# The last stage's products as seven half-size block products instead of eight

## The reference, cut to what matters

```
def _sage_layer(h, edge_src, edge_dst, deg_inv, W_self, W_neigh, b):
    msg = h[edge_src]
    agg = segment_sum(msg, edge_dst, num_segments=h.shape[0])
    return h @ W_self + (agg * deg_inv[:, None]) @ W_neigh + b
...
h   = relu(_sage_layer(x, ..., W_self0, W_neigh0, b0))
out =      _sage_layer(h, ..., W_self1, W_neigh1, b1)
x   = _layernorm(x + out)
```

## Time and profile before

| | |
|---|---|
| median of the runs | 1059.83 us |
| profiled execution | 1060.87 us |
| its span, first to last instruction | 1059.1 us |
| TensorE busy | 999.0 us, 94% |
| VectorE busy | 516.8 us, 49% |
| ScalarE busy | 370.5 us, 35% |
| GpSimd busy | 262.4 us, 25% |
| mean granted TensorE clock | 0.983 |

### The profile page before, as it was taken

How to read it: one execution, slowest core, us unless ns; L and a number is a source line. 1 busy time by engine, 2 the same in 40 slices (tenths; PEclk the granted TensorE clock), 3 DMA queues, 4 the chain that set the end, 5 groups by cost and what they waited for, 6 DMA issues and landing times.

```text
span 1059.1 us, 14881 instructions
## 1 busy us (share of the span) xinstructions
PE 999.0 (94%) x4870; PEld 810.8 (77%) x4870; DVE 516.8 (49%) x1296; ACT 370.5 (35%) x664; POOL 262.4 (25%) x320
## 2 busy tenths in 40 slices
PE   5798899989898999999999999999999999999996
PEld 3376678879787887877777777778887777787774
DVE  7888765374667885332223332212234233235545
ACT  5687743162535576221112221113431101222221
POOL 3000003841443331633006143006116004300000
PEclk9699999999999999999999999999999999999999
DMA  6158683893013684314224014324325435104443
GB/s 204 58 97 216 171 196 73 199 204 86 0 42 121 230 287 143 104 34 149 96 75 126 22 47 135 106 104 140 114 83 159 131 109 163 29 1 132 146 146 123
DMA packets 48263, 127.13 MB, mean 120 GB/s; under 512 B 17775, under 2 KB 18784, under 8 KB 48016
## 3 DMA queue, kind: packets, MB, share of 16 engines
q1 hardware_dynamic: 33622, 74.91, 23.6%
q0 software_dynamic: 8288, 37.29, 13.3%
q10 hardware_dynamic: 6298, 14.21, 3.9%
HBM read 101.76 MB, written 45.13 MB: 139 GB/s over the span
## 4 chain that ended last, share of the span: by engine, by line
PE 77%; DVE 11%; ACT 5%; issue 3%; POOL 1%; DVEq 0%; ACTq 0%; POOLq 0%
PE bank L1778 42%; PE bank L1799 18%; PE bank L1117 6%; PE bank L1149 4%; PE bank L663 3%; PE bank L627 2%; DVE hot_keys L444 2%; ACT squares L1347 1%; DVE hot_src L443 1%; DVE dec_z L1430 1%; PE bank L1491 1%; DVE xt L475 1%; PE bank L620 1%; PE bank L1176 1%; PE bank L1476 1%
## 5 line engine op out<-in xcount | busy, mean ns | idle before, releaser
L1718 DVE TENSOR_TENSOR h_stage<-h_turned,h_stage 128x1000 fp32r<-128x1000 f32 x80 | 104.6, 1307 | 370.6 <-ACT h_stage L1643 370.6
L1778 PE MATMUL bank<-w_self,h_stage 128*125 128x512 f32 x960 | 229.5, 394 | 0.0
L1778 PE MATMUL bank<-w_neigh,h_stage 128*125 128x512 f32 x960 | 227.2, 397 | 0.0
L1778 PEld LDWEIGHTS bank<-w_self,h_stage 128*125 128x125 f32 x960 | 177.8, 185 | 45.0
L1778 PEld LDWEIGHTS bank<-w_neigh,h_stage 128*125 128x125 f32 x960 | 178.0, 186 | 43.9
L1799 PE MATMUL bank<-g_rows,a_stage 125*125 125x512 f32 x800 | 192.7, 395 | 0.0
L1643 ACT ACTIVATE h_stage<-h_turned 128x1000 fp32r (+1 forms) x80 | 84.0, 1050 | 304.6 <-PE bank L1778 293.0
L1799 PEld LDWEIGHTS bank<-g_rows,a_stage 125*125 125x125 f32 x800 | 148.4, 185 | 37.8
L1608 POOL CAST w_self<-w_stage 128x512 fp32r<-128x512 f32 x32 | 22.2, 695 | 226.3 <-PE bank L1778 218.9
L1149 PE MATMUL bank<-a_turned,gn 125*128 125x418 f32 x360 | 70.8, 354 | 3.9 <-DVE gn L1009 2.4
L1149 PEld LDWEIGHTS bank<-a_turned,gn 125*128 125x128 f32 x360 | 66.9, 188 | 5.7 <-DVE gn L1009 3.6
(11 more groups left out here) (217 smaller groups left out, 1122.6 us busy)
## 6 DMA issues: line engine op xcount, KB each, us to landing
a_stage<-at_dram SPq DMA_DIRECT2D x40, 625.0 KB, 4.0
w_stage<-w_self POOLq DMA_DIRECT2D x32, 256.0 KB, 3.1
at_dram<-a_turned SPq DMA_DIRECT2D x10, 625.0 KB, 9.6
w_stage<-w_neigh POOLq DMA_DIRECT2D x24, 256.0 KB, 2.9
dec_y<-x_bd SPq DMA_DIRECT2D x10, 512.0 KB, 3.7
dec_x<-x_ob SPq DMA_DIRECT2D x10, 512.0 KB, 4.6
x_dram<-h_rows SPq DMA_DIRECT2D x10, 512.0 KB, 2.9
h_dram<-o ACTq DMA_DIRECT2D x20, 256.0 KB
```

What stands on the lines that cost most here:

```text
L1718: dve.tensor_tensor(st[u][:, 1, :, :], ht[:, :, bass.ds(t * NT, NT)], raw(st[u][:, 0, :, :]), ALU.subtract).then_inc(st_ready, 1)
L1778: mm = pe.matmul(out, st[u][:, a, k, :], w[:, b, k * 512:(k + 1) * 512], start=(k == 0 and p == 0), stop=(k == KD - 1 and p == 2))
```

## The change

For one quarter, write h in row halves (tiles 0 to 4, tiles 5 to 9) and column halves (input blocks 0 to 3 and 4 to 7), and [W_self | W_neigh] in halves of its 1024 input rows. h times that matrix, 2 x 2 blocks by 2 x 2 blocks, is eight block products. The change computes it by seven (Winograd's form), with sums of node blocks and of weight blocks ahead and combinations of the results behind:

- A job is one row tile of one block product: 4 x 3 = 12 matmuls. `JOBS` is the order, 35 of them a quarter; product numbers 1, 2, 6, 7, 4 one after the other, then 5 and 3 interleaved. Then ten aggregations follow, tile after tile, without products between them.
- VectorE makes the node sums (`first_sums`, `third_sum`, `fourth_sum`, `first_sum_again`), the stage's low halves (128 x 500), the weight sums (`weight_sums`) and, instead of GpSimd, the weights' low halves; ScalarE their high halves. VectorE combines the results out of PSUM (`evict`) into `e`, `u2` and `o`; `o` is now kept for all ten tiles, so the self product is complete ahead of the aggregations.
- A quarter reads 44 pieces of weights instead of 16, through a ring of five buffers. Two sums are stored to DRAM (`t1_dram`, `t2_dram`) and loaded again later. GpSimd only issues these loads; `freed` says what each waits for.
- Each set of weights has one of three places; sets 1 and 2 of the next quarter are made during the aggregations (`tile_sets`).
- In the last quarter the rows are normalized in place (in `res` and `o`) and stored from there, and the load of `res` waits for landed stores.

```diff
+    PLAIN = [(prod, r) for prod in (1, 2, 6, 7, 4) for r in range(HT)]
+    PAIRED = [(5, 0), (5, 1), (3, 0), (5, 2), (3, 1), (5, 3), (3, 2), (5, 4), (3, 3), (3, 4)]
+    JOBS = PLAIN + PAIRED
+    RING = 5
...
+        def load_residual(q, t):
+            u, hf = t % 2, q % 2
+            if t < 2:
+                sp.wait_ge(g_lo, 10 * q + (5, 9)[t])
+                if q == 3:
+                    sp.wait_ge(o_out[u], out_count(3, u))
+            elif q == 2:
+                sp.wait_ge(o_resid, t - 1)
+            else:
+                sp.wait_ge(o_out[u], out_count(3, u) + 32 * (t // 2))
+            sp.dma_start(res[u][:, 0, :], io["x2_dram"][t, :, 512 * hf:512 * hf + 512]).then_inc(res_in[u], 16)
+            if q == 3:
+                sp.dma_start(res[u][0:NT, 1, :], io["y_dram"][t, 0:NT, :]).then_inc(res_in[u], 16)
...
+        def freed(n):
...
+                    if w % SETS == 2 and j in (0, 2):
+                        pool.wait_ge(t_out, OUT0 + 32 * (HK * (w // SETS) + k + 1))
+                    if j == 1:
+                        pool.wait_ge(w_sum, SUM0 + sum_order(w, k) + 1)
+                    elif not (w % SETS == 2 and j == 0):
+                        pool.wait_ge(w_lo, LO0 + halves_order(w, k) + 1)
...
+                for j, source in enumerate(sources):
+                    n = pieces_until(w, k) + j
...
+                    freed(n - RING)
+                    load(n, source)
...
+        def weight_high(w, k):
...
+            act.activation(slots[w % 3][:, 0, k, :], source[:, :], ACT.Copy).then_inc(w_hi, 1)
+            if i == 2:
+                act.dma_start(io["t1_dram"][q, k], piece[pieces_until(w, k) % RING][:, :]).then_inc(t_out, 16)
+                act.dma_start(io["t2_dram"][q, k], source[:, :]).then_inc(t_out, 16)
...
+        def finish(q, t):
+            u = t % 2
+            if q == 3:
...
+                for y in (res[u][0:NT, 1, :], o[t][0:NT, :]):
+                    act.activation(y, y, ACT.Identity, bias=f_sh[u][0:NT, :], scale=f_rs[u][0:NT, :]).then_inc(f_normed, 1)
+                act.wait_ge(f_normed, NORMED0 + 2 * t + 2)
+                act.dma_start(io["out"][t * NT:(t + 1) * NT, 0:512], res[u][0:NT, 1, :]).then_inc(o_out[u], 16)
+                act.dma_start(io["out"][t * NT:(t + 1) * NT, 512:D], o[t][0:NT, :]).then_inc(o_out[u], 16)
+                return
...
+        def weight_sums(w, k):
...
+            first = piece_of(dve, w, k, 0)
+            second = piece_of(dve, w, k, 1)
+            dve.tensor_tensor(first[:, :], first[:, :], second[:, :], ALU.subtract).then_inc(w_sum, 1)
+            if i == 2:
+                third = piece_of(dve, w, k, 2)
+                dve.wait_ge(w_sum, SUM0 + sum_order(w, k) + 1)
+                dve.tensor_tensor(third[:, :], third[:, :], first[:, :], ALU.subtract).then_inc(w_sum, 1)
...
+        def at_job(q, i):
+
+            if i > HT:
+                evict(q, i - 1)
+            if i + 2 < NJ:
+                stage_low(q, i + 2)
...
+            if i > 0:
+                for w, k in quarter_sets(q, i - 1):
+                    weight_low(w, k)
+            for w, k in quarter_sets(q, i):
+                weight_sums(w, k)
...
+            biased(q, 0)
+            for t in range(T):
+                if t + 1 < T:
+                    biased(q, t + 1)
+                finish(q, t)
+                if t > 0:
+                    for w, k in tile_sets(q, t - 1):
+                        weight_low(w, k)
+                for w, k in tile_sets(q, t):
+                    weight_sums(w, k)
+                if t >= T - 2 and q < 3:
+                    stage_low(q + 1, t - T + 2)
...
+    def job(q, i):
...
+                for p, (a, b) in enumerate(HALVES):
+                    mm = pe.matmul(bank(q, i)[0:NT, :], st[m % 3][:, a, k, :], slots[w % 3][:, b, k, :],
+                                   start=(k == 0 and p == 0), stop=(k == HK - 1 and p == 2))
+            mm.then_inc(p_done, 1)
```

More of the change, by code:

```diff
@@ L1312, in _ @@
                 store(t - 3)
-        for layer in range(2):
-            sp.dma_start(s.sage_bias[:, layer, :], io["sage_b"][layer:layer + 1, :].to_broadcast([128, D]))\
-              .then_inc(s.bias_in, 16)
         for t in range(T - 3, T):
@@ L1537, in _, with tile_sets, made @@
+    def tile_sets(q, t):
+        return [(SETS * (q + 1) + n, k) for n, first in ((1, 0), (2, 4)) for k in range(HK) if first + k == t]
+    def made(w):
+        return w < SETS * len(QUARTERS)
     @block.sync
@@ L1615, in through, with load @@
-    def through(eng, phase, stage, tile):
-        with eng.Fori(1 if phase == 0 else 0, HF - 1) as i:
-            for u in range(2):
-                stage(phase, i + 1, u)
-                tile(phase, i, u)
-        for u in range(2):
-            if phase + 1 < len(PHASES):
-                stage(phase + 1, 0, u)
-            tile(phase, HF - 1, u)
+        def load(n, source):
+            pool.dma_start(piece[n % RING][:, :], source).then_inc(piece_in[n % RING], 16)
+        def freed(n):
+            if n < 0:
+                return
+            for w in range(FIRST_SET, SETS * 4):
+                for k in range(HK):
+                    j = n - pieces_until(w, k)
+                    if not 0 <= j < (1, 1, 3, 2, 2, 1, 1)[w % SETS]:
+                        continue
+                    if w % SETS == 2 and j in (0, 2):
[4 more added lines that the diff above has]
+                        pool.wait_ge(w_lo, LO0 + halves_order(w, k) + 1)
@@ L1767, in _ @@
     @block.tensor
     def _(pe):
-        def turn(i, u):
-            t = 2 * i + u
-            pe.wait_ge(rows_in[u], 16 * i + 16)
-            pe.wait_ge(ht_ready, 2 * t + 1)
-            turn_rows(pe, s, u)
-        def product(out, u, w):
-            for k in range(KD):
-                for p, (a, b) in enumerate(HALVES):
-                    mm = pe.matmul(out, st[u][:, a, k, :], w[:, b, k * 512:(k + 1) * 512],
-                                   start=(k == 0 and p == 0), stop=(k == KD - 1 and p == 2))
-            return mm
@@ new lines, in _ @@
+        pe.wait_ge(s.y_read, 2 * (T - 1))
+        for q in range(4):
+            for i in range(NJ):
+                if q == 0 and i == 2:
+                    pe.wait_ge(s.y_read, 2 * T)
+                job(q, i)
+                if q == 0 and i == 0:
+                    s.turn_x2(pe, T - 2)
+                if q == 0 and i == 2:
+                    s.turn_x2(pe, T - 1)
+                if q == 2 and i == 1:
+                    turn(T - 1)
+            for t in range(T):
+                aggregate(q, t)
+                if q == 1 and t > 0:
+                    turn(t - 1)
```

618 lines of the change are left out of this document (379 added, 239 removed).

## The result

The changed kernel takes 1212.33 us (median of four runs, 1209.52 to 1214.41) against 1060.62 (1059.80 to 1061.42): a ratio of 1.1436, 95% interval 1.1414 to 1.1458. The forecast was 1144, range to 1178: slower, as said, but by 152 us and not by 84. The profiled execution took 1212.87.

What follows compares the result with a forecast made beforehand. TensorE, busy 94% of the span, was taken to bound the kernel. The terms, -55.6 for saved matmuls against chiefly +84.6 tail and +25 junctions, summed to +84.4 on 1060.87, 1145.3, or 1144 us as a median; range 1114 to 1178.

Steps and rivals of the forecast that it cites:

- The matmuls saved: All four quarters: 240 fewer product matmuls on TensorE at 0.2315 us each, -55.6 us.
- the start: Start of the last stage: only job 0 stands ahead of row tile 8's turn, 12 matmuls lose their cover, +2.8 us.
- the first quarter: First quarter's products: weight pieces waiting for stored sums delay job 10, +9 us; the weight-sum loop slows later jobs, +6.
- the gap from products to aggregation: Each quarter's first aggregation waits for VectorE to evict job 34 and make a low half: +1.4 x 4 = +5.6 us.
- the later quarters' jobs: Products of the three later quarters: lag from the weight-sum loop, +2 us, from 0 to 18.
- Rival (b): Last quarter's tail not serial, residual in time: VectorE sets 5.5 us a tile, +8 instead of +84.6; 1068 us, chance 0.06.
- the tail's store at 3.85 and load at 4.2: Last quarter's tiles: store and residual load times in a serial cycle of 15.1 us a tile, +84.6 us.
- 17.7 a tile: Last quarter's tail, upper end: store 4.1 and load 6.3 us, making the tail term +105.
- junctions at +25: Aggregations between quarters: next quarter's weight sums delay job 0, by 9.0 us, 7.3 in quarter 1; +25 over three.
- 40, if a cycle takes 10 us: Upper end of the three junctions' term, since a tile there also brings 625 KB of counts.
- the turns use part of the wait: Junction in quarter 1: turns of 0.86 us each fill some of the wait, 7.3 us instead of 9.0.
- The clock: After each junction's wait TensorE's granted clock drops for a while: 3 x 1.7, +5 us; nothing in the tail.

Runs made afterwards that it cites:

- e3: Changed kernel, with VectorE's bias and residual of tile t+1 moved behind the combination of tile t in the last quarter: 1151.49 us.
- e4: Changed kernel, with a place of its own for each tile's residual in the last quarter, so no load waits for a store: 1124.38 us.
- e7: Changed kernel with own residual places, all 125-row transfers cut into 120 and 5, six ring buffers and later ScalarE weight halves: 1070.83 us, ratio 1.0103 to the kernel before.
- e8: On top of e1, only a tenth of the counts of tiles 2 to 9 loaded in the first three quarters (timing only): 1150.85 us.
- e1: Changed kernel, with each 125-row transfer of the tail cut into 120 and 5 rows: 1167.65 us.
- e10: Changed kernel with e1, e4, six ring buffers, later ScalarE weight halves, earlier weight sets, row loads behind counts, stage halves ahead of finish: 1059.54 us.
- e12: On top of e10, a third buffer for the counts: 1039.79 us, ratio 0.9826 to the kernel before.

## Why the prediction was wrong

**The sign and the mechanism held.** The matmuls saved, the start, the first quarter (121.8 for 122.7), the gap from products to aggregation (1.5 us, job end 685.2 to aggregation 686.7) and the later quarters' jobs (4.6 over in three) came out as worked out. Of the 4.6 most is the third quarter's, 105.9 us where the others took 100.5 and 101.9: its first jobs stand behind the second junction's last turn, and at 772.97 TensorE had waited 2.38 us for a stage's low half. The first quarter is no luck of the sum, as its sums, its job 10 and its loop each came at their time. The tail was serial over exactly the links named, and e3 and e4 show that both of its conditions, VectorE's order and the load behind landed stores, were needed. Rival (b), a residual in time, wanted another order of the buffers, and became true in e7.

**The step that failed first: the tail's store at 3.85 and load at 4.2.** They were priced from transfers of another shape. The store (820.80 to 824.49) is a single one of 128 rows, 256 KB. In the tail two are issued 0.3 us apart, with 125 rows each: 5.93 us behind the second issue, DMA share 0.29 to 0.31, and 2.22 when cut into 120 and 5 rows. The load took 5.54, with 4.2 taken, against a median of 4.9 in the earlier trace rows that I argued down; those loads had 128 rows as well, so their 4.9 against the 3.0 of the weight loads is not from the row count, and even this median was too low. 8 x 3.7 = 30 of the tail's 33.7. The upper end of that term, 17.7 a tile, was itself too low, since its store (4.1) is that of the old form, 120 and 5 rows, which the change gave up. The diff held this, and the forecast took the transfers as unchanged.

**The second: junctions at +25.** They cost 55.6. e8 takes away 17.0 with the counts' bytes alone, of 30.6 missing here and 27.0 in e1, on which it is built. So pieces and stores crowded by 625 KB a tile were priced too low; the range's "40, if a cycle takes 10 us" had the right reason, with 9.6, 11.2 and 9.8 us a cycle measured at the three. Another 6 are the second quarter's order: "the turns use part of the wait" was wrong. In ScalarE's queue the relu of tile 7 and the copy of tile 6's turn stand behind the last weight's high half, so tile 7's turn waits for the sum, and aggregation 9 stands behind that turn, in series. That was to be read from the two queues; here it is read from two chains (this kernel's and e8's), and no run tests it alone. The third junction has the residual's wait besides, which no term covers; part of it goes with the counts' bytes too (8.9 us of waits in e8 from 860 to 895). Some 7 stay unassigned, in e1 some 4, and that is within the 7.1 us by which the sum of the junctions differs between kernels that don't differ there.

**The clock**, +5: 0.66, 1.00 and 0.50 (1.2 GHz throughout) granted in the first 4 us behind the junctions, so 1.4, 0 and 2.0 us, 3.4 in all. The lower level lay partly inside the junctions instead: aggregation 9 of the second took 6.03 us for 20 matmuls and not 4.66, with 0.73 granted from 756.5 to 762.5, after TensorE had been idle for 3.3 us.

**The range** left out that both sizes rest on the same thing, the landing time of a transfer under company. It was the case in which the terms are wrong together, and the two upper ends added (+20 and +15) would have said 1180; even that isn't enough.

**What stays open.** Ring, schedule and bytes, each by itself, took 18.4, 12 and 17 us off the junctions, 47 in sum, where the forecast was 30.6 short, so each is in part a remedy for the same wait; in e7 and e10 only the joint effect of their edits is shown. The third buffer is shown by itself, as e12 differs from e10 only by it and the waits that go with it. That the row count sets a transfer's time is shown by three cuts and their DMA shares; the number of engines behind it is not on any record here. Whether the tail at 5.5 can go to TensorE's 4.66 with VectorE's order changed as well wasn't tried.

## What to carry to other kernels

When a change makes a transfer part of a cycle, take its price from a transfer of the same number of rows, the same neighbours and the same count in flight, and put the doubt of all such prices into the range together. Read the diff for what it does to the transfers' shapes: the row counts that e1 puts back look like a detail and were worth 45 us here. Ask of each load how long ahead its buffer comes free: a third buffer turned a kernel at par into one 1.7% faster without a byte less. And follow an in-order queue beyond the instruction that waits: a relu behind a weight's half, a turn behind the relu, aggregation 9 behind the turn.

## What was not expected of the hardware

While two stores of 125 rows and 250 KB each run, the DMA engines are busy to a share of 0.29 to 0.31, and they land 5.93 us behind the second issue. Cut into 100 and 25 rows they land 3.60 us behind the last issue, at a share of 0.42; cut into 120 and 5 rows, 2.22 us behind it, at 0.62 to 0.74. And loads of the same 625 KB took 4.0 us in the kernel before, 5.8 in the changed one and 8.7 in the tail of e4_resbuf (medians), by what ran beside them.
